# A Perceiver layer pair on one core: the first feed-forward as one program that reads 16-bit integers, the first cross attention merged with the norm of its latents, its tail keys on two halves of the array

## The chip, the cores and the metric

The kernel runs on one core of a Trainium2 chip. The metric is the device time of one execution in microseconds, as the median of several runs. Five engines take part: TensorE (PE in the profile, its weight loads PEld), VectorE (DVE), ScalarE (ACT), GpSimd (POOL) and SyncE (SP), which here only issues transfers.

## The reference, cut to what matters

The input x has 128 batches of 32 tokens with 128 features, the context 128 batches of 257 rows of 128. Six blocks follow one another, each added to x:

```python
x = x + L0_xattn(ctx, layernorm(x), mask)     # 16 heads of 64, keys = context AND latents
x = x + L0_attn(layernorm(x))                 # gated linear recurrence
x = x + L0_ffn(layernorm(x))                  # feed-forward with quantised activations
x = x + L1_xattn(layernorm(x), ctx, mask)     # 16 heads of 8
x = x + L1_attn(layernorm(x))
x = x + L1_ffn(layernorm(x))                  # experts and a shared expert
```

The two that the change touches:

```python
# first cross attention: the latents are normalised again and appended to the context
kv = concatenate([layer_norm(ctx, g1, b1), layer_norm(latents, g2, b2)], axis=1) @ Wkv   # 257 + 32 keys
weight = softmax(where(mask, q @ k.T * 64**-0.5, -big));  out = (weight @ v) @ Wout

# first feed-forward
def act_qdq(x):                                # one scale for the whole tensor
    scale = max(max(abs(x)) / 32767, 1e-12)
    return clip(round(x / scale), -32768, 32767) * scale
x = act_qdq(x)
up, gate = act_qdq(x @ wu.T), act_qdq(x @ wg.T)        # 128 -> 384
sig = clip(round(sigmoid(gate) * 65536), 0, 65535) / 65536
gate = act_qdq(gate * sig);  o = act_qdq(gate * up)
return o @ wd.T                                        # 384 -> 128
```

Each `act_qdq` needs the maximum over everything before the first element can be rounded, so the feed-forward has four points at which all work waits for one number.

## The kernel before

The tokens lie in a tile x of 128 partitions and 32 tiles of 128 features; a chunk is 4 tiles (512 columns), so there are 8 chunks. The stages run one after the other. Each stage is one or several blocks; in a block every engine has a program of its own, ordered by semaphores, and at a block's end all engines meet.

**First cross attention, `xattn0`.** It begins with `xattn0_inputs` (L448): `ln_stats` (L74) computes mean and scale for the 32 tiles and for the context's last row, as a block of its own. A second block then goes over the 8 chunks: VectorE and ScalarE normalise two tiles each (L480, L528), TensorE turns them and ScalarE writes `latT` (L534); VectorE multiplies by g2 (L486), GpSimd adds b2 (L501), and SyncE stores the result to memory (L557), from where it comes back as values. Then the block of the attention starts. GpSimd clears five tiles there (L681 to L686) and VectorE waits for that. Every engine next runs `step(g, j)` for each batch (`run_steps`, L431): 7 lead-in steps, the first 8 batches written out, a loop over 14 groups of 8 batches, the last 8 batches written out. A step works on several batches at once, for instance scores for batch s + 3 and values for batch s.

Per batch TensorE computes the scores (L853: 4 groups of 4 heads, 3 passes, 290 columns), a quarter of the next queries (L879), the product of probabilities and values over two context key tiles (L863) and over the third tile of keys, the tail (L870: the 32 latents and the last context row, spread over 128 partitions, most of them zero), and two transposes (L907). Every fourth batch it projects a finished tile (L895). VectorE masks the scores and takes the minimum (L728), transposes the probabilities in 32x32 blocks (L739 the two context tiles, L741 the tail), and does the context's norm (L755, L762, L769) and low halves (L773, L786). ScalarE takes the exponential and normalises (L801, L809) and copies out of PSUM (L819, L834, L838). GpSimd does scale and shift of the norm (L694 to L702) and, once a tile, the keys of the tail and the mask's bias (L709 to L716). SyncE spreads the transposed blocks over the partitions (L648, 4 transfers a batch) and loads raw context (L635) and tail values (L665, L667).

**First feed-forward, `ffn0`** (L1223). It is a chain of blocks, most of them with loops. (a) `layer_norm_T` (L136): VectorE normalises, TensorE turns, ScalarE copies into yT. `tensor_scale` (L1180) takes the maximum over all 4096 columns (L1196), turns it into a row, and forms step and inverse. (b) ScalarE multiplies by the inverse and adds the rounding constant RNE (L1259), VectorE takes it off and multiplies by the step (L1294), the result is split in a high and a low part (L1270, L1321), TensorE forms gate and up in 3 passes (L1332), ScalarE copies them (L1278), VectorE takes maxima (L1301). (c) Per item of 1024 columns, 12 items: ScalarE scales the gate (L1350), GpSimd subtracts RNE (L1370), ScalarE takes the sigmoid (L1356), VectorE rounds it (L1381), multiplies (L1385) and takes the maximum (L1389). (d) ScalarE scales up and gate (L1411, L1412), GpSimd subtracts RNE from up (L1421), VectorE multiplies (L1429) and takes the maximum (L1434). (e) ScalarE scales (L1457), VectorE dequantises (L1480), TensorE multiplies by the down weights (L1508), ScalarE copies, TensorE turns back (L1520), VectorE adds to x (L1488) and takes statistics.

## Time and profile before

| | before |
|---|---|
| runs, us | 1985.6, 1988.06, 1990.55; median 1988.06 |
| profiled execution, us | 1983.28 (span 1981.5) |
| PE / PEld busy | 1701.8 (86%) / 1391.9 (70%) |
| DVE / ACT / POOL busy | 1593.8 (80%) / 1490.9 (75%) / 889.3 (45%) |
| mean granted TensorE clock | 0.927 of 2.4 GHz |
| DMA | 261.67 MB, mean 132 GB/s |

Busy times are sums over the span. As the stages follow one another and differ in what leads them, a share of the whole says little; the stretches of the section on rows are cut at the stages. In timelines the first number is the start in us from the span's beginning, the second the length of the piece, and brackets hold the idle time before it and what ended it. Matmul pieces overlap by their tails, so the distance from start to start is what one costs.

### The profile page before, as it was taken

Reading aid. Unit: us, or ns where it says so; the run is one execution under the profiler, and the core shown is the slowest. Engines: PE = TensorE matmul, PEld = TensorE weight load, DVE = VectorE, ACT = ScalarE, POOL = GpSimd, SP = SyncE. Lnnn points to the kernel's source line nnn. Section 1 sums busy time; section 2 is a strip of 40 time slices with the busy share of each in tenths; the row PEclk is TensorE's granted clock in tenths of the full one; section 3 lists DMA queues with packets and bytes.
Section 4 is the critical chain, followed back from the end, with each engine's and each line's share of the span. In section 5 each row is a group of like instructions: output and inputs, shape, how many; then the busy total and the mean of one; then the engine's idle time right before and its main releaser. Section 6 shows DMA issues by size and latency. Waiting matters only on the chain. (4 is left out here: it accounts for less than half of the span.)

```text
span 1981.5 us, 50909 instructions
## 1 busy us (share of the span) xinstructions
PE 1701.8 (86%) x13415; PEld 1391.9 (70%) x13415; DVE 1593.8 (80%) x5006; ACT 1490.9 (75%) x4152; POOL 889.3 (45%) x1335
## 2 busy tenths in 40 slices
PE   3599999999999999985530569999999889979997
PEld 3499999999999999973420246676666556667775
DVE  4798888888888888849688779999999778866664
ACT  3588888888888888857576469999999778855553
POOL 1654444444444444412145224444444367725554
PEclk8699999999999999997675789999999889969998
DMA  4366666666666666640000039999999710016555
GB/s 139 94 167 163 161 161 161 161 161 161 161 161 161 161 162 162 162 114 0 0 0 0 0 102 247 252 250 249 249 249 249 194 33 0 1 28 100 102 96 107
DMA packets 224924, 261.67 MB, mean 132 GB/s; under 512 B 25144, under 2 KB 178268, under 8 KB 224720
## 3 DMA queue, kind: packets, MB, share of 16 engines
q1 hardware_dynamic: 223366, 258.64, 52.9%
q10 hardware_dynamic: 1194, 1.58, 0.3%
q8 instruction: 33, 0.54, 0.1%
q0 software_dynamic: 288, 0.56, 0.1%
q14 instruction: 43, 0.35, 0.1%
HBM read 88.19 MB, written 4.74 MB: 47 GB/s over the span
## 5 line engine op out<-in xcount | busy, mean ns | idle before, releaser
L863 PE MATMUL a_out<-a_probT,a_xn 128*128 128x256 f32 x1024 | 264.5, 382 | 4.2 <-DMA a_probT<-a_blocks 3.4
L801 ACT ACTIVATE a_prob<-a_neg,a_nmax 128x289 f32<-128x289 f32 x512 | 266.8, 526 | 1.3 <-DVE a_nmax L728 1.0
L694 POOL TENSOR_TENSOR a_xn<-a_z,g 128x256 f32<-128x256 f32 x128 | 94.0, 734 | 383.9 <-DVE a_z L762 383.9
L1767 ACT ACTIVATE b_prob<-b_neg,b_nmax 128x257 f32<-128x257 f32 x512 | 259.6, 512 | 5.8 <-DVE b_nmax L1702 5.1
L853 PE MATMUL a_score<-a_xnT,a_qT 128*128 128x290 f32 x1536 | 252.6, 314 | 1.1 <-DVE a_qT L773 1.1
L728 DVE CUSTOM_DVE_ANT_0 a_neg<-a_score,a_bias 128x289 f32<-128x289 f32 x512 | 211.4, 457 | 39.9 <-PE a_score L853 35.7
L809 ACT ACTIVATE a_prob<-a_prob,a_rinv 128x289 f32<-128x289 f32 x512 | 231.3, 528 | 1.8 <-DVE a_rinv L778 1.8
L853 PEld LDWEIGHTS a_score<-a_xnT,a_qT 128*128 128x128 f32 x1536 | 221.9, 190 | 7.9 <-issue 1.4
L1702 DVE CUSTOM_DVE_ANT_0 b_neg<-b_score,b_bias 128x257 f32<-128x257 f32 x512 | 188.4, 418 | 24.4 <-PE b_score L1872 17.0
L863 PEld LDWEIGHTS a_out<-a_probT,a_xn 128*128 128x128 f32 x1024 | 176.3, 192 | 19.2 <-DMA a_probT<-a_blocks 4.4
L739 DVE STREAM_TRANSPOSE a_blocks<-a_prob 128x1024 f32<-128x1024 f32 x128 | 159.4, 1245 | 22.5 <-ACT a_prob L809 16.0
L2438 POOL TENSOR_TENSOR m_hidden<-m_full,m_hidden 128x512 fp32r<-128x512 f32 (+1 forms) x88 | 113.7, 1292 | 109.1 <-ACT m_hidden L2397 109.1
L1713 DVE STREAM_TRANSPOSE b_blocks<-b_prob 128x1024 f32<-128x1024 f32 x128 | 156.4, 1222 | 1.2 <-ACT b_prob L1767 0.7
L879 PE MATMUL a_q<-latT,A 128*128 (+1 forms) x1024 | 139.5, 280 | 12.9 <-DVE a_qT L773 10.6
L879 PEld LDWEIGHTS a_q<-latT,A 128*128 128x128 f32 x1024 | 130.6, 196 | 14.7 <-DVE a_qT L773 12.0
L870 PE MATMUL a_out<-a_probT,a_tail 128*128 128x256 f32 x512 | 131.4, 379 | 0.0
L819 ACT ACTIVATE a_oT<-a_out 128x512 f32<-128x512 f32 x128 | 76.5, 598 | 71.6 <-PE a_out L870 71.6
L2392 ACT ACTIVATE m_silu<-m_g 128x512 f32<-128x512 f32 (+1 forms) x88 | 52.6, 597 | 92.1 <-PE m_g L2161 92.0
L895 PE MATMUL a_ctx<-U,a_oT 128*128 128x128 f32 x1024 | 119.7, 275 | 0.7 <-ACT a_oT L819 0.7
L895 PEld LDWEIGHTS a_ctx<-U,a_oT 128*128 128x128 f32 x1024 | 116.9, 192 | 1.1 <-ACT a_oT L819 1.1
L1673 POOL TENSOR_TENSOR b_last_part<-b_v_rows,b_prob 128x128 f32<-128x128 f32 x128 | 52.0, 406 | 129.0 <-ACT b_prob L1767 129.0
L870 PEld LDWEIGHTS a_out<-a_probT,a_tail 128*128 128x128 f32 x512 | 97.3, 190 | 13.2
(484 smaller groups left out, 4520.9 us busy)
## 6 DMA issues: line engine op xcount, KB each, us to landing
a_probT<-a_blocks SPq DMA_DIRECT2D x512, 192.0 KB, 3.4
b_probT<-b_blocks SPq DMA_DIRECT2D x256, 256.0 KB, 4.6
a_raw<-in_ctx SPq DMA_DIRECT2D x128, 128.0 KB, 3.0
b_raw<-in_ctx SPq DMA_DIRECT2D x64, 256.0 KB, 4.2
m_wide<-expert_weights SPq DMA_DIRECT2D x128, 128.0 KB, 6.8
a_kept<-keep SPq DMA_DIRECT2D x32, 257.0 KB, 3.4
b_kept<-keep SPq DMA_DIRECT2D x32, 257.0 KB, 4.7
b_v_rows<-ctx_tail_values SPq DMA_DIRECT2D x32, 256.0 KB, 4.7
```

The source lines that it names most:

```text
L728: nc.vector.tensor_tensor_reduce(out=neg[:, grp, :], in0=score_ps[grp][:, 0:KEYS0], in1=bias[:, n, :], scale=-DH0 ** -0.5, scalar=3.4e38, ...
L739: nc.vector.transpose(blocks[:, n, :, 0:2].rearrange("p r t g l -> p g r t l"), prob[:, n, :, 0:2 * P].rearrange("p g (r t c) -> p g r t c ...
L801: nc.scalar.activation(prob[:, par, grp, 0:KEYS0], neg[:, grp, :], ACT.Exp, bias=nmax[:, par, grp:grp + 1], scale=-1.0, accum_out=rsum[:, ...
L809: last = nc.scalar.activation(part, part, ACT.Copy, scale=rinv[:, j % 2, grp:grp + 1])
L853: last = nc.tensor.matmul(score_ps[grp][:, 0:even(KEYS0)], qT[:, a, un, bn, 4 * grp:4 * grp + 4, :], xnT[:, c, n, :], start=(p == 0), stop ...
L863: nc.tensor.matmul(out_ps[:, half, 0:2 * P], xn[:, j, kt, :], probT[:, u, 2 * half:2 * half + 2, kt, :], start=(kt == 0), stop=False)
L870: last = nc.tensor.matmul(out_ps[:, half, 0:2 * P], tail[:, j, :], probT[:, j % 2, 2 * half:2 * half + 2, 2, :], start=False, stop=True)
L879: last = nc.tensor.matmul(q_ps[:, h * P:(h + 1) * P], k.A[:, 4 * hg + h, :], k.latT[:, ds((t + ahead) * P, P)], start=True, stop=True)
L895: last = nc.tensor.matmul(proj_ps, oT[:, slot, :], k.U[:, slot % GROUPS * HG + slot // GROUPS, :], start=(slot == 0), stop=(slot == H - 1))
L1702: nc.vector.tensor_tensor_reduce(out=neg[:, par, grp, :], in0=score_ps[grp][:, 0:N_CTX], in1=bias[:, n, :], scale=-DH1 ** -0.5, scalar=3.4 ...
L1713: nc.vector.transpose(blocks[:, n, :, j % 2].rearrange("p r t g l -> p g r t l"), prob[:, j % 4, :, 0:2 * P].rearrange("p g (r t c) -> p g ...
L1767: nc.scalar.activation(prob[:, (j + 5) % 4, grp, :], neg[:, par, grp, :], ACT.Exp, bias=nmax[:, par, grp:grp + 1], scale=-1.0, accum_out=r ...
```

## The change

1. **Tail keys on two halves.** The 33 tail keys stand twice, in partitions 0 to 63 and again in 64 to 127, the latents in two rows of every four. One half of the partitions serves each half of the heads, so both tail matmuls of a batch contract over 64 rows, each in its own half of the array. Both kinds of value matmuls now take as their columns 64 of each of 4 head blocks. VectorE transposes the tail's probabilities in two instructions of 192 elements with overlapping windows instead of one of 256, SyncE loads the tail tile with 5 transfers instead of 2. The slots of the heads in the projection follow (U's index).
2. **The norm of the latents inside the attention's block.** `xattn0_inputs` is gone. `ln_stats` takes a SyncE and a GpSimd program along (the first raw loads; the clearing, now of a third of `blocks`). The chunk work stands written out ahead of the steps, with four of the seven lead-in steps between chunks 1, 3, 5 and 7; its tiles lie in `oT`, its PSUM in `out_ps`.
3. **VectorE's loop placed.** `run_steps` can say where in the instruction memory the loop's first instruction stands; VectorE's of this stage stands at slot 0.
4. **The feed-forward as one block**, written out without loops. Where the rounded value was needed, engines read the low 16 bits of the 32-bit word (value plus RNE) as an integer; the passes that took RNE off are gone, except in part (b), where GpSimd does it for chunks 1 to 7. The step is applied where the products are copied (b) and at the end (e). Maxima are taken chunk by chunk; half of up's scaling moves into (c); the sigmoid's table is loaded ahead. In (e) the activations are the stationary operand, so the product comes out in x's layout, with no copy and no turning back.

```diff
-def run_steps(eng, step, lead, lag=0, rest=8):
+def run_steps(eng, step, lead, lag=0, rest=8, **place):
-    with eng.Fori(1, (B - rest) // 8) as g:
+    with eng.bass.Fori(1, (B - rest) // 8, engines=[eng.engine], **place) as g:
...
+        EARLY = {1: 1, 3: 2, 5: 3, 7: 4}
+        mean, root, twice = ln_stats(k, stack, "lat_ln", k.ctx_tail[:], first_loads, clear)
...
-                        sp.dma_start(tail[0:P:KEY_STEP, rows, :], k.lat_dram[...]).then_inc(tail_loaded[u], 16)
+                        for first in (0, P // 2):
+                            for r in range(2):
+                                sp.dma_start(tail[first + r:first + P // 2:KEY_STEP, rows, :], latents[r * (L // 2):(r + 1) * (L // 2)])\
+                                    .then_inc(tail_loaded[u], 16)
+                        sp.dma_start(tail[2:P:P // 2, rows, :], k.ctx_tail_dram[batches, :].unsqueeze(0).broadcast_to([2, BPT, D]))\
                             .then_inc(tail_loaded[u], 16)
...
+                sp.wait_ge(tail_scaled, 2)
+                sp.dma_start(k.ctx_tail_dram, last_row[:, 1, :]).then_inc(tail_stored, 16)
+                for c in range(CHUNKS):
+                    sp.wait_ge(affine_ready, c + 1)
+                    sp.dma_start(k.lat_dram[c * CH:(c + 1) * CH, :].rearrange("(t p) d -> p t d", p=P), lat[:, c % 2]).then_inc(stored[c % 2], 16)
+                sp.wait_ge(z_ready, 1)
+                load_raw(sp, 0, 4)
+                for u in range(2):
+                    sp.wait_ge(stored[u], CHUNKS // 2 * 16)
+                run_steps(sp, step, LEAD - 2)
...  (GpSimd)
+                for c in range(CHUNKS):
+                    pool.wait_ge(lat_scaled, c + 1)
+                    nc.gpsimd.tensor_tensor(lat[:, c % 2], lat[:, c % 2], wide4(k.b2), ALU.add).then_inc(affine_ready, 1)
+                    if c in EARLY:
+                        step(-1, EARLY[c])
+                pool.wait_ge(lat_copied, CHUNKS)
+                run_steps(pool, step, LEAD - len(EARLY))
...  (VectorE)
-                    nc.vector.transpose(blocks[:, n, 0:2, 2].rearrange("p r g l -> p g r l"),
-                                        prob[:, n, :, 2 * P:2 * P + 2 * L].rearrange("p g (r c) -> p g r c", c=L)).then_inc(blocks_ready, 1)
+                    for half in range(2):
+                        pair = slice(2 * half, 2 * half + 2)
+                        last = nc.vector.transpose(blocks[:, n, 0:3, 2, pair].rearrange("p r g l -> p g r l"), tail_windows(n, half))
+                    last.then_inc(blocks_ready, 1)
...
+                    last.then_inc(z2_ready, 1)
+                    wait(dve, stored[u], c // 2 * 16)
+                    dve.wait_ge(z2_ready, c + 1)
+                    dve.wait_ge(z2_act, c + 1)
+                    nc.vector.tensor_tensor(lat[:, u], z2[:, u], wide4(k.g2), ALU.mult).then_inc(lat_scaled, 1)
...
+                run_steps(dve, step, LEAD - len(EARLY), LAG, head_slot={dve.engine: 0})
...  (TensorE)
-                        nc.tensor.matmul(out_ps[:, half, 0:2 * P], xn[:, j, kt, :], probT[:, u, 2 * half:2 * half + 2, kt, :],
+                        nc.tensor.matmul(out_ps[:, half, 0:2 * P], xn[:, j, kt, :], probT[:, u, :, kt, half * (P // 2):(half + 1) * (P // 2)],
...
-                        last = nc.tensor.matmul(out_ps[:, half, 0:2 * P], tail[:, j, :], probT[:, j % 2, 2 * half:2 * half + 2, 2, :],
-                                                start=False, stop=True)
+                        part = slice(half * (P // 2), (half + 1) * (P // 2))
+                        last = nc.tensor.matmul(out_ps[:, half, 0:2 * P], tail[part, j, :], probT[part, j % 2, :, 2, part], start=False, stop=True)
...  (ffn0, new)
+        def low(t):
+            return t.bitcast(I16).rearrange("p (n two) -> p n two", two=2)[:, :, 0]
...  ScalarE
+                def sigmoid(n):
+                    wait(act, gs_ready, n - SLOTS + 1)
+                    act.wait_ge(g_scaled, n + 1)
+                    nc.scalar.activation(part[:, n % SLOTS, :], low(item(all_gate, n)), ACT.Sigmoid, scale=step_of(UG, 1)).then_inc(sig_ready, 1)
...
+                for c in ACT_SCALES[1:]:
+                    scale_y(c)
+                for c in range(CHUNKS):
+                    if c + 1 < CHUNKS:
+                        upper_half(c + 1)
+                    for n, t, ps, w in sides:
+                        for j in range(FB0):
+                            act.wait_ge(done[n], c * FB0 + j + 1)
+                            nc.scalar.activation(chunk(t[:, j], c), ps[j][:], ACT.Copy, scale=step_of(Y)).then_inc(copied[n], 1)
+                nc.scalar.activation(sig_table[:], k.zero[:], ACT.Sigmoid)
+                act.wait_ge(scale_ready, UG + 1)
+                scale_gate(0)
+                scale_gate(1)
+                for n in range(ITEMS):
+                    sigmoid(n)
+                    if n + 2 < ITEMS:
+                        scale_gate(n + 2)
+                    if n % 2:
+                        scale_up(n // 2)
...  GpSimd
+                for c in range(1, CHUNKS):
+                    pool.wait_ge(y_hi, c + 1)
+                    nc.gpsimd.tensor_tensor(chunk(yT, c), chunk(yT, c), k.minus_rne[:].broadcast_to([P, CH]), ALU.add).then_inc(y_clean, 1)
+                    pool.wait_ge(y_clean, c)
+                    nc.gpsimd.tensor_tensor(y[:, LO, c * CH:(c + 1) * CH], chunk(yT, c), y[:, HI, c * CH:(c + 1) * CH], ALU.subtract)\
+                        .then_inc(y_lo, 1)
...  VectorE
+                def multiply_gate(n):
+                    dve.wait_ge(sig_rounded, n + 1)
+                    nc.vector.scalar_tensor_tensor(item(all_gate, n), part[:, n % SLOTS, :], -SIG, low(item(all_gate, n)), ALU.add, ALU.mult)\
+                        .then_inc(gs_ready, 1)
...
+                    nc.vector.tensor_tensor(item(all_up, n), low(item(all_gate, n)), low(item(all_up, n)), ALU.mult).then_inc(o_ready, 1)
...
+                    nc.vector.tensor_scalar(o, low3(o), step_of(O), None, ALU.mult).then_inc(o_dve, 1)
...  TensorE
+                def down(c):
+                    pe.wait_ge(o_dve, c + 1)
+                    pe.wait_ge(o_act, c + 1)
+                    wait(pe, added, c - 2)
+                    for n in range(4):
+                        t = c * 4 + n
+                        for j in range(FB0):
+                            last = nc.tensor.matmul(up_ps[c % 3][:, n * P:(n + 1) * P], up[:, j, t * P:(t + 1) * P], k.f_down[:, j, :],
+                                                    start=(j == 0), stop=(j == FB0 - 1))
```

## Rows read from the trace of the kernel before

**Rows 1.** Busy time by stretch: PE, PEld, DVE, ACT, POOL (instructions), then clock.
```profile
38.60:103.70 65.10, 34.75 (x165) 29.08 (x166) 47.38 (x147) 35.88 (x87) 35.27 (x55) 0.61 0.31 88
110.00:860.00 750.00, 749.73 (x5062) 706.02 (x5061) 646.94 (x2350) 622.64 (x1814) 351.87 (x662) 1.00 0.66 161
946.00:968.10 22.10, 9.21 (x33) 5.91 (x33) 16.03 (x48) 5.00 (x9) 0.00 (x0) 0.50 0.00 1
968.10:1013.30 45.20, 35.45 (x146) 28.58 (x146) 34.64 (x31) 37.64 (x66) 10.31 (x8) 0.88 0.00 0
1013.30:1066.30 53.00, 0.48 (x1) 0.18 (x1) 44.85 (x43) 28.54 (x25) 27.25 (x12) 0.50 0.00 0
1066.30:1109.10 42.80, 0.48 (x1) 0.18 (x1) 35.52 (x33) 27.27 (x24) 31.95 (x12) 0.50 0.00 0
1109.10:1144.70 35.60, 28.23 (x80) 13.29 (x80) 22.61 (x48) 17.33 (x16) 0.00 (x0) 0.88 0.00 1
```

**Rows 2.** Timeline of TensorE in the first attention's loop: start, length, operation.
```profile
506.69 1.03 PE L870 MATMUL a_out<-a_probT,a_tail 128*128 128x256 f32 x4
507.37 1.97 PE L853 MATMUL a_score<-a_xnT,a_qT 128*128 128x290 f32 x12
...
512.69 2.00 PE L853 MATMUL a_score<-a_xnT,a_qT 128*128 128x290 f32 x12
...
520.73 3.74 PE L895 MATMUL a_ctx<-U,a_oT 128*128 128x128 f32 x32
```

**Rows 3.** Timeline of TensorE in the second attention's loop.
```profile
1302.15 0.72 PE L1835 MATMUL b_score<-b_kT,b_qbd 32*128 32x257 f32 x8
1302.80 0.70 PE L1856 MATMUL b_k<-b_turned_in,wk1T 128*128 128x256 f32 x2
1303.33 0.38 PE L1864 MATMUL b_in<-ident,b_raw 128*128 128x128 f32 x2
```

**Rows 4.** Timeline of TensorE in the setup, two products of 64 rows.
```profile
26.98 0.27 PE L410 MATMUL setup_ps<-wk0T,wq0T 64*128 64x128 f32 x1
26.98 0.27 PE L410 MATMUL setup_ps<-wout,wv0T 64*128 64x128 f32 x1
```

**Rows 5.** Timeline of VectorE in the first attention's loop.
```profile
510.18 1.25 DVE L739 STREAM_TRANSPOSE a_blocks<-a_prob 128x1024 f32<-128x1024 f32 x1 [0.19 <-ACT a_prob L809]
511.35 0.40 DVE L741 STREAM_TRANSPOSE a_blocks<-a_prob 128x256 f32<-128x256 f32 x1
...
524.62 0.29 DVE L782 TENSOR_TENSOR x<-a_ctx,x 128x128 f32 x1 [0.50 <-PE a_ctx L895]
```

**Rows 6.** Timeline of GpSimd before the first attention's loop.
```profile
59.05 1.31 POOL L501 TENSOR_TENSOR lat_affine<-lat_affine,b 128x512 f32<-128x512 f32 x1 [0.95 <-DVE lat_affine L486]
...
76.35 0.29 POOL L709 CAST a_xnT<-latT 128x128 fp32r<-128x128 f32 x1
...
78.74 0.72 POOL L694 TENSOR_TENSOR a_xn<-a_z,g 128x256 f32<-128x256 f32 x1
...
83.77 0.71 POOL L702 TENSOR_TENSOR a_rstd<-a_var,minus_half 128x2 f32<-128x2 f32 x1
```

**Rows 7.** Timeline of VectorE in the first feed-forward.
```profile
962.12 4.42 DVE L1196 TENSOR_REDUCE f_y_scale<-f_yT 128x1 f32<-128x4096 f32 x1 [2.39 <-PEq L144]
...
1041.24 1.25 DVE L1381 TENSOR_SCALAR f_part<-f_part 128x1024 f32<-128x1024 f32 x1
1042.41 1.21 DVE L1385 SCALAR_TENSOR_TENSOR f_gate<-f_part,f_gate 128x1024 f32 x1
...
1054.41 0.68 DVE L1381 TENSOR_SCALAR f_part<-f_part 128x1024 f32<-128x1024 f32 x1
...
1077.43 1.78 DVE L1429 SCALAR_TENSOR_TENSOR f_up<-f_gate,f_up  x1
```

**Rows 8.** Timeline of TensorE in the first feed-forward.
```profile
973.32 4.14 PE L1332 MATMUL f_up<-f_y,f_w_up 128*128 x9 [5.99 <-POOL f_y L1321]
...
1112.71 7.62 PE L1508 MATMUL f_down<-f_up,f_downT 128*128 x12 [4.84 <-DVE f_up L1480]
```

More of the change, by code:

```diff
@@ L1358, in _, with norm @@
-                for n in range(-2, 3):
-                    step(n, n % 3)
-                with act.Fori(1, ITEMS // 3 - 1) as g:
-                    for u in range(3):
-                        step(g * 3 + u, u)
-                for n in range(ITEMS - 3, ITEMS):
-                    step(n, n % 3)
+                def norm(c):
+                    for j in (2, 3):
+                        t = c * 4 + j
+                        last = nc.scalar.activation(z[:, t * D:(t + 1) * D], k.x[:, t * D:(t + 1) * D], ACT.Identity,
+                                                    bias=offset[:, t:t + 1], scale=rstd[:, t:t + 1])
+                    last.then_inc(z_act, 1)
@@ new lines, in _ @@
+                act.wait_ge(inv_ready, 1)
+                nc.scalar.activation(rstd[:], inv[:], ACT.Sqrt).then_inc(root_ready, 1)
+                act.wait_ge(offset_ready, 1)
+                norm(0)
+                norm(1)
+                for c in range(CHUNKS):
+                    act.wait_ge(turned, c + 1)
+                    nc.scalar.activation(chunk(yT, c), ln_ps[c % 2][:], ACT.Copy).then_inc(yT_copied, 1)
+                    if c + 2 < CHUNKS:
+                        norm(c + 2)
@@ new lines, in statistics @@
+                def statistics(c):
+                    dve.wait_ge(added, c + 1)
+                    for n in range(4):
+                        last = tile_stats(k, c * 4 + n)
+                    last.then_inc(x_stats_ready, 1)
+                norm_chain()
+                for c in range(CHUNKS):
+                    norm(c)
+                    if c >= 2:
+                        max_y(c - 2)
+                max_y(CHUNKS - 2)
+                max_y(CHUNKS - 1)
+                dve.wait_ge(y_maxed, CHUNKS)
@@ new lines, in _ @@
+                find_scale(Y, y_max[:].unsqueeze(1))
+                dve.wait_ge(scale_ready, Y + 1)
+                scale_y(DVE_SCALES[0])
+                dve.wait_ge(y_hi, 1)
+                nc.vector.tensor_tensor(y[:, LO, 0:CH], low(chunk(yT, 0)), y[:, HI, 0:CH], ALU.subtract).then_inc(y_lo0, 1)
+                for c in DVE_SCALES[1:]:
+                    scale_y(c)
+                for c in range(CHUNKS):
+                    max_side(0, c)
+                    max_side(1, c)
+                dve.wait_ge(maxed, 2 * CHUNKS)
@@ L1512, in _, with turn @@
[L1512 to L1521 removed]
+                def turn(c):
+                    pe.wait_ge(z_ready, c + 1)
+                    pe.wait_ge(z_act, c + 1)
+                    wait(pe, yT_copied, c - 1)
+                    for j in range(4):
+                        t = c * 4 + j
+                        last = nc.tensor.transpose(ln_ps[c % 2][:, j * P:(j + 1) * P], z[:, t * D:(t + 1) * D], k.ident[:])
+                    last.then_inc(turned, 1)
@@ new lines, in turn_rows, with products @@
+                def turn_rows(i):
+                    pe.wait_ge(chain[i], 2)
+                    for t in range(scale[i].shape[2]):
+                        last = nc.tensor.transpose(rows_ps[:, t * P:(t + 1) * P], rows[:, t, :], k.ident[:])
+                    last.then_inc(rows_turned, 1)
+                def products(c):
+                    if c == 0:
+                        pe.wait_ge(w_lo, 2)
+                        pe.wait_ge(y_lo0, 1)
+                    else:
+                        pe.wait_ge(y_lo, c)
+                    for n, t, ps, w in sides:
+                        for j in range(FB0):
+                            wait(pe, copied[n], (c - 1) * FB0 + j + 1)
+                            for p, (a, b) in enumerate(PASSES):
+                                last = nc.tensor.matmul(ps[j][:], w[:, a, j * P:(j + 1) * P], y[:, b, c * CH:(c + 1) * CH],
+                                                        start=(p == 0), stop=(p == len(PASSES) - 1))
+                            last.then_inc(done[n], 1)
@@ L1524, in xattn1 @@
+                for c in range(CHUNKS):
+                    turn(c)
+                turn_rows(Y)
+                for c in range(CHUNKS):
+                    products(c)
+                turn_rows(UG)
+                turn_rows(GS)
+                turn_rows(O)
+                for c in range(CHUNKS):
+                    down(c)
 def xattn1(k, io):
```

712 lines of the change are left out of this document (302 added, 410 removed).

## Prediction

> **What bounds the kernel now.** I read the page's slices first, then the windows by stage, and in each stage the timeline of the engine without gaps. The profiled execution took 1983.28 us around a span of 1981.5; 4.8 us below the median of the runs shown (1988.06), so I work out a difference and take it from the median. The reader should see three stages [rows 1]. From 38.6 to 103.7 nothing is full: the latents' norm is a program of its own, with the attention's lead-in behind it. From 110 to 860 TensorE is busy 749.73 of 750 us at the 2.4 GHz level: the first attention's loop is TensorE's. From 946.0 to 1144.7 lies the first feed-forward, five stretches in which VectorE or ScalarE leads, TensorE only in the second and last.
>
> In the loop a batch takes 5.32 us (score to score, 507.37 to 512.69), and every fourth has 32 projection matmuls as well, 3.74 with the tail of the last, 3.57 without it, so 0.112 each [rows 2]: 24.85 us a tile of four batches, 32 tiles. VectorE is close behind: per ordinary batch it waits only 0.2 for ScalarE, so its own work is about 5.17; once a tile it waits 0.50 and more [rows 5].
>
> **Part 1, tail keys on two halves (TensorE).** Now: 4 instructions (2 matmuls, 2 instructions each, as all f32 here) of 0.216, from 506.69; the fourth streams until 507.55: 0.86 us a batch [rows 2]. After: the two matmuls hold 64 rows each, in different row groups. That such streams run side by side shows in the setup, where two 64-row products start together at 26.98 [rows 4]. So the stretch has two rounds, 2 x 0.216 = 0.43. But the shape changes twice. The second attention does that each batch: eight 32-row instructions of 257 columns take 0.65 from their start to the next start (1302.15 to 1302.80), two rounds of 0.217 plus 0.21 of weight load and emptying; the 128-row pair behind them takes 0.53 to its successor where two cost 0.43 [rows 3], 0.10 for its bare weight load. What the entry costs beyond the stretch's own first load no row gives alone; I take 0.08, an emptying like the one behind it. Sum 0.65 + 0.10 + 0.08 = 0.83 against 0.86: 0.03 saved, times 128 = -4 us. Bounds: no entry cost, 0.75 (-14 us); entry as dear as load and emptying together, 0.95 (+11). 0.83 lies nearest to the rows.
>
> The page "TensorEngine Tiling (Array Packing)" of the Trainium skill (Key Properties) says that changing the mode drains TensorE, while its section Theoretical Speedup gives up to 2x for a contraction of 64. By the 2x alone a batch would save 0.43; but then VectorE (below) holds ordinary batches at 5.36 and the loop gains 9 us, not 4. By the drain, the trace agrees, 0.1 and a bare weight load per change [rows 3].
>
> **VectorE's share.** The 256-element transpose (0.40) becomes two of 192. From the 1024 one (1.25) and the 256 one, an element costs 1.11 ns and an instruction 0.12, of which some 0.07 overlaps the next [rows 5]: 2 x 0.26 instead of 0.33, +0.19. Its ordinary batch is then 5.36, above TensorE's 5.29, and it falls behind 0.07 a batch; three batches make 0.2, with its own 0.19 some 0.4, against the 0.50 it waits before the tile's addition [rows 5]. So it catches up once a tile and costs nothing; cover 0.1 us a tile. Below: nothing gained, as TensorE leads. Above: the lag isn't recovered, rival A. Where VectorE's loop starts in its instruction memory changes no row I can price: no gap stands at the loop's edge; 0, up to 1 us in each of 14 turns either way.
>
> SyncE issues five tail loads a tile for two, some 0.5 us each more, 1.5 us, in the batch before the projection, where it has 8.9 us for four instructions of spreading, some 0.7 each by estimate; the bytes go from 66 to 132 KB per 24.85 us, beside 161 GB/s [rows 1]. Hidden; if not, the loads of raw context come 1.5 late with several us in hand.
>
> **Part 2, the latents' norm merged.** Now POOL adds a bias for 8 chunks (1.31 each, with a pause of 0.95 before it), then clears tiles, and only then does the lead-in begin; POOL ends its fourth lead-in step at 83.77 + 0.71 = 84.48 [rows 6]. After: the clearing lies beside the statistics chain, and four steps lie between the chunks. POOL becomes the merged block's bound: from 46.95, 8 x 1.30 = 10.4; four variance-and-power pairs at 0.95 = 3.8; three products-and-sums at 1.5 = 4.5; the tile keys from 76.35 to 78.74, 2.4 [rows 6]; waits on VectorE 1.5. It ends at 69.6 instead of 84.5: -15. TensorE's cold clock (0.5 for most of this stage) hurts less than POOL. Late next is SyncE: its tail loads and the fifth raw tile wait until the last latents are stored, about 69.4, so raw 5 lands near 75.5, just when it is wanted. Bounds: -17 (VectorE's own chain), -11 (SyncE late by 4).
>
> **Part 3, the feed-forward.** The integers are read as the low 16 bits, so neither POOL nor VectorE takes the rounding constant away; five blocks become one.
> (a) 946.0 to 968.1, 22.1 us: the 4.42 reduction over 4096 elements becomes a maximum per chunk, of which the last 0.6 stays, and the 2.39 before it shrinks by a block's edge, 1.2 [rows 7]. -4.9.
> (b) 45.2 us: the first product starts at 973.32, after 5.99 idle [rows 8]; then it stands 2.2 after the scale, for 5.2 now. The 144 matmuls behind it are TensorE's (busy 35.45 of 45.20 [rows 1]) and stay, 16 groups of nine; ScalarE's copies take the scale along free, its chunk about 3.8 < 4.08, POOL's now two passes 2.5. With the edge: -4.1.
> (c) 53.0 us: POOL's subtraction goes. Where it runs, VectorE's rounding takes 1.25, and with the product and the maximum at 1.17 + 2 x 1.13 = 3.43 an item; where it has ended the same takes 0.68, so 2.86 [rows 7] (an instruction of 1.21 frees the engine after 1.13: 1041.24 + 1.17 = 1042.41). Then 12 x 2.86 = 34.3, filling 6.9 (ScalarE: two scalings, sigmoids in line), scale 2.2: 43.4. ScalarE per item, an estimate from its 28.54 busy for 25 instructions [rows 1], 1.13 + 1.06 + half of a 1.13 scaling of up = 2.75, under VectorE's. -9.6.
> (d) 42.8 us: the product took 1.78 beside POOL; free it is 1.13, as is the maximum [rows 7]. 12 x 2.26 = 27.1, start 1.3, scale 2.4: 30.8. ScalarE, 27.27 busy for 24 of its scalings now [rows 1], has 18, 20.4, hidden. -12.0.
> (e) 35.6 us: no copy and no turning back; 24 instructions a chunk at 0.112 = 2.69, VectorE by my estimate 1.13 + 0.6 + 0.82 = 2.55. 8 x 2.69 = 21.5; 2.9 to the first product, 2.0 lost at the 1.2 GHz level until the clock rises (it rose 4.5 us after 1112.71 [rows 8]), 1.5 at the end: 27.9. -7.7.
> Sum -38.3. The trace of before has no 16-bit read with stride: below, nothing gained over f32; above, half rate on 24 products (+25, rival B). I take the f32 rate, that of the same elements. Bounds without that: -31 (fills and scales 1.5 longer in each part), -44 (ScalarE and VectorE overlap fully).
>
> **Sum.** -4 - 15 - 38.3 = -57.3: 1983.3 becomes 1926.0, and on the median 1930.8, say 1930. Its own range: 1988 - 75 = 1913 to 1988 - 31 = 1957, rarely at both ends together; 1914 to 1950.
>
> **Rivals.**
> A. VectorE becomes the loop's bound: ordinary batches at 5.44 and the lag carried over. For it: 0.1 us of cover a tile. Against: waits of over 1 us behind the addition in the projection batch. Tile 3 x 5.44 + 8.88 = 25.20, +0.35 x 32 = +11 instead of -4: 1946.
> B. The strided 16-bit reads run at half rate: +1.07 on 24 products and some on the last stretch: 1961. For it: no row. Against: no element more is read.
> C. The merged start is bound elsewhere (SyncE's wait for the stores, ScalarE's alternate work): 5 saved for 15: 1940.
> D. Slower: the two halves don't overlap on the same accumulation, and both shape changes cost 0.32 (the 0.21 of load and emptying and the 0.10 of a bare load, together, at each). The tail stretch is 0.86 + 0.64 = 1.51, +0.65 x 128 = +83, less 53: 2018. It decides from 1.28 us a stretch. Against it: rows 3 and 4.
> E. The change does less than it says: POOL leaves the feed-forward, but VectorE's rounding stays at 1.25. Then (c) saves 3, not 9.6: 1937.
>
> **Chances.** Forecast 0.60, A 0.16, C 0.09, E 0.05, B 0.06, D 0.04. The range 1910 to 1952 holds the forecast's own, A, C and E, leaving B, D and tails out. Faster by over 0.3% (6 us, about what a measurement of this kernel tells from none) 0.93, within it 0.03, slower 0.04.
>
> **What would show it.** Tail stretch, values' end to first score: near 0.83; near 0.5 means no drain, above 1.28 D. TensorE full from about 95 to 855, a tile 24.7; if VectorE is full and TensorE has gaps in the loop, A. Lead-in's fourth POOL step ends near 70. Feed-forward 199 to about 160, VectorE's rounding 0.68 throughout, its product 1.2 (B: 2.3). Wrong: a loop turn above 50.5 us, or a feed-forward above 172.

## The result and the profile after

The changed kernel took 1940.21 us (median of 4 runs, 1938.02 to 1943.30), the kernel before 1988.30 in the same session. The ratio is 0.976 with a 95% interval of 0.9741 to 0.9778: 48 us faster, where 58 were forecast. Both the profiled executions lie below their medians, 1938.02 (span 1936.2) and 1983.28 (span 1981.5), 45.3 apart.

The ends of the blocks on VectorE cut both spans into stages:

| stage | before | after | difference | forecast |
|---|---|---|---|---|
| setup, to 37.2 / 36.6 | 37.2 | 36.6 | -0.6 | 0 |
| first attention, to 889.5 / 876.4 | 852.3 | 839.8 | -12.5 | -19 |
| recurrence, to 944.9 / 932.5 | 55.4 | 56.1 | +0.7 | 0 |
| first feed-forward, to 1144.7 / 1096.5 | 199.8 | 164.0 | -35.8 | -38.3 |
| second attention, to 1587.8 / 1539.9 | 443.1 | 443.4 | +0.3 | 0 |
| second recurrence, to 1743.9 / 1696.1 | 156.1 | 156.2 | +0.1 | 0 |
| second feed-forward, to the end | 237.6 | 240.1 | +2.5 | 0 |

The same stretches as in [rows 1], first the attention's start, then its loop, then the five parts (a) to (e) of the feed-forward (busy time of PE, PEld, DVE, ACT, POOL with their instructions, then clock, DMA share, GB/s):

```profile
36.60:93.00 56.40, 32.12 (x167) 28.28 (x168) 44.79 (x141) 34.50 (x80) 34.61 (x54) 0.66 0.32 92
110.00:840.00 730.00, 730.00 (x4970) 627.46 (x4969) 645.28 (x2421) 614.98 (x1771) 344.77 (x650) 1.00 0.67 164
932.50:951.90 19.40, 8.94 (x33) 5.99 (x33) 14.22 (x41) 11.76 (x27) 1.95 (x2) 0.50 0.00 0
951.90:993.80 41.90, 35.52 (x146) 28.38 (x146) 31.29 (x26) 38.80 (x63) 16.34 (x14) 0.91 0.00 1
993.80:1037.05 43.25, 0.47 (x1) 0.18 (x1) 36.06 (x43) 33.06 (x30) 0.00 (x0) 0.50 0.00 0
1037.05:1067.86 30.81, 0.47 (x1) 0.18 (x1) 28.73 (x33) 20.48 (x18) 0.00 (x0) 0.50 0.00 0
1067.86:1096.50 28.64, 23.75 (x192) 23.59 (x192) 17.38 (x49) 18.36 (x16) 0.00 (x0) 0.88 0.00 1
```

TensorE is busy 730.00 of 730 us: the loop is still its own, so rival A (VectorE sets its pace) did not come. GpSimd is gone from (c) and (d). In the loop, TensorE's timeline (start, length) answers to [rows 2] and VectorE's to [rows 5]:

```profile
501.35 0.70 PE L847 MATMUL a_out<-a_probT,a_tail 64*128 64x256 f32 x4
501.98 1.86 PE L829 MATMUL a_score<-a_xnT,a_qT 128*128 128x290 f32 x12
...
507.25 1.88 PE L829 MATMUL a_score<-a_xnT,a_qT 128*128 128x290 f32 x12
...
516.10 1.88 PE L829 MATMUL a_score<-a_xnT,a_qT 128*128 128x290 f32 x12
```

```profile
510.07 1.25 DVE L675 STREAM_TRANSPOSE a_blocks<-a_prob 128x1024 f32<-128x1024 f32 x1 [0.16 <-ACT a_prob L767]
511.24 0.59 DVE L679 STREAM_TRANSPOSE a_blocks<-a_prob 128x192 f32<-128x192 f32 x2
...
513.74 0.29 DVE L720 TENSOR_TENSOR x<-a_ctx,x 128x128 f32 x1 [0.23 <-PE a_ctx L871]
```

A batch takes 507.25 - 501.98 = 5.27 for 5.32, so rival D (0.65 more a batch) did not come either. A turn of eight takes (828.56 - 137.05) / 14 = 49.39 for 49.71. VectorE's wait before the tile's addition fell from 0.50 to 0.23: it falls behind a little in each ordinary batch and has caught up by the end of the tile.

GpSimd ahead of the loop (its fourth lead-in step ends at 74.91 + 0.71 = 75.62; [rows 6] had 84.48) and VectorE there:

```profile
55.11 1.30 POOL L645 TENSOR_TENSOR a_oT<-a_oT,b 128x512 f32<-128x512 f32 x1 [2.51 <-DVE a_oT L745]
...
74.91 0.71 POOL L619 TENSOR_TENSOR a_rstd<-a_var,minus_half 128x2 f32<-128x2 f32 x1
```

```profile
53.05 0.69 DVE L711 TENSOR_TENSOR a_qT<-a_q,a_qT 128x512 fp32r<-128x512 f32 x1 [2.02 <-ACT a_qT L792]
53.65 0.59 DVE L739 TENSOR_SCALAR a_oT<-x,lat_ln_mean,lat_ln_twice 128x128 f32<-128x128 f32 x2
...
75.43 0.46 DVE L658 CUSTOM_DVE_ANT_0 a_neg<-a_score,a_bias 128x289 f32<-128x289 f32 x1 [1.06 <-issue]
```

In the feed-forward, VectorE answers to [rows 7] and TensorE to [rows 8]:

```profile
1005.62 0.68 DVE L1419 TENSOR_SCALAR f_part<-f_part 128x1024 f32<-128x1024 f32 x1
1006.22 1.22 DVE L1423 SCALAR_TENSOR_TENSOR f_gate<-f_part,f_gate 128x1024 f32<-128x1024 f32 x1
1007.35 1.21 DVE L1428 TENSOR_REDUCE f_gs_max<-f_gate 128x1 f32<-128x1024 f32 x1
1008.48 0.68 DVE L1419 TENSOR_SCALAR f_part<-f_part 128x1024 f32<-128x1024 f32 x1
...
1039.57 1.22 DVE L1433 TENSOR_TENSOR f_up<-f_gate,f_up 128x1024 f32<-128x1024 int16 x1
```

```profile
954.28 4.18 PE L1536 MATMUL f_up_ps<-f_y,f_w_up 128*128 128x512 f32 x9 [3.09 <-DVE f_y L1467]
958.26 2.47 PE L1536 MATMUL f_gate_ps<-f_y,f_w_gate 128*128 128x512 f32 x9
960.57 2.20 PE L1536 MATMUL f_up_ps<-f_y,f_w_up 128*128 128x512 f32 x9
...
1070.46 23.75 PE L1547 MATMUL f_up_ps<-f_downT,f_up 128*128 128x128 f32 x192 [3.81 <-DVE f_up L1442]
```

The item is 1008.48 - 1005.62 = 2.86, as forecast.

### The profile page after: what moved, and what is told of

The parts are those of the page before. It is cut to its first block and busy times, and to the rows that moved or that the text cites. A ratio compares the mean times of both kernels' runs of the same rounds, so it can differ in the third digit from the quotient of the medians.

```text
span 1936.2 us, 50375 instructions
## 1 busy us (share of the span) xinstructions
PE 1690.7 (87%) x13527; PEld 1332.0 (69%) x13527; DVE 1581.4 (82%) x5121; ACT 1505.8 (78%) x4166; POOL 837.8 (43%) x1319
## 5 line engine op out<-in xcount | busy, mean ns | idle before, releaser
L829 PE MATMUL a_score<-a_xnT,a_qT 128*128 128x290 f32 x1536 | 241.4, 306 | 1.2 <-DVE a_qT L711 1.1
L829 PEld LDWEIGHTS a_score<-a_xnT,a_qT 128*128 128x128 f32 x1536 | 210.9, 189 | 42.7 <-issue 42.7
L1806 ACT ACTIVATION_READ_ACCUMULATOR b_prob<-b_neg,b_nmax 128x1 f32 x512 | 104.6, 204 | 0.0
L2031 POOL TENSOR_TENSOR s_spread<-s_keys,head_of_feature 128x1536 f32<-128x1536 f32 x32 | 88.8, 2776 | 34.7 <-ACT s_keys L2125 34.7
```

Source lines behind the costliest of these rows:

```text
L829: last = nc.tensor.matmul(score_ps[grp][:, 0:even(KEYS0)], qT[:, a, un, bn, 4 * grp:4 * grp + 4, :], xnT[:, c, n, :], start=(p == 0), stop ...
L1806: nc.scalar.activation(prob[:, (j + 5) % 4, grp, :], neg[:, par, grp, :], ACT.Exp, bias=nmax[:, par, grp:grp + 1], scale=-1.0, accum_out=r ...
```

## The experiments

All are edits of the changed kernel. Where it says "in one run", the kernel ran once, with the profiler; the others have 4 or 5 runs. Where a stage is given, it is from the profiles. Most stages repeat far better than whole runs: where its code is unchanged the feed-forward took 163.3 to 165.2 us. The second attention, whose code is the same everywhere, took 441.9 to 451.4, so whole times that differ by a few us say little.

**1. Without the placement of VectorE's loop.**

```diff
-                run_steps(dve, step, LEAD - len(EARLY), LAG, head_slot={dve.engine: 0})
+                run_steps(dve, step, LEAD - len(EARLY), LAG)
```

> The changed kernel without the placement of VectorE's loop in the first attention. My theory: the loop is TensorE's (730.00 of 730 us busy from 110 to 840), VectorE catches up once a tile, so the time stays at 1938 to 1943, a turn of 8 batches stays 49.39 (two tiles of 24.68 or 24.70), and at most a gap of under 1 us appears on VectorE at the loop's edge. Rival: the placement is what made a turn 0.32 shorter than before (49.71); then a turn is 49.7 here and the time 5 us longer.

Measured: 1976.56 us (1974.36 to 1979.41), 36 us longer. Both my theory and its rival were wrong: it is far more than either. What VectorE waited for from 190 to 830 (total, times, longest), and the place in one turn:

```profile
DVE a_neg L658 <- issue: 38.8, 13, 3.7
```

```profile
501.55 0.17 DVE L716 RECIPROCAL a_rinv<-a_rsum 128x4 f32<-128x4 f32 x1
501.63 0.39 DVE L724 TENSOR_TENSOR a_xnT<-a_ctx,a_xnT 128x256 fp32r<-128x256 f32 x1
505.12 0.46 DVE L658 CUSTOM_DVE_ANT_0 a_neg<-a_score,a_bias 128x289 f32<-128x289 f32 x1 [3.09 <-issue]
```

Thirteen gaps of 3.0 on average, with no releaser: 14 turns have 13 jumps back. The trace's records of the jump itself show where the time goes: the next instruction of VectorE's sequencer starts 3.4 to 4.2 us behind each jump back, and the two instructions shown ahead of the gap had been issued before the jump. In the changed kernel, and in the one before, it starts 0.3 to 0.4 behind. The changed kernel has no line of "issue" in that stretch. A turn lasts 51.7 to 54.0 us for 49.39: VectorE cannot make up for it in two tiles, and TensorE waits for its masks.

**2. The loop at slot 236** (`head_slot={dve.engine: 236}` for 0).

> The changed kernel with VectorE's loop placed at slot 236 instead of slot 0. Without any placement VectorE stood still for 2.8 to 3.7 us once in each turn, just behind the loop's edge, with nothing it waited for that the profile shows, and the time was 36 us longer. The body has 283 instructions, in the kernel before it had 275. Theory: what counts is whether the body lies in two or in three stretches of 256 slots; from 236 it ends at 518, in the third, so the gap is back: 14 gaps of about 3 us, 30 to 40 us longer, 1970 to 1980. Rival (any stated placement helps, by the branch that it puts ahead of the loop or by a better entry): no gaps, 1938 to 1943.

Measured in one run: 1984.23 us; the gaps are back (13 of them, 35.6 us in all), and a turn is (875.4 - 139.0) / 14 = 52.60, 3.2 more. The theory holds, its price was set somewhat low. A second, smaller gap appears inside the body in 9 of the turns, some twenty instructions behind its first, about where slot 256 lies:

```profile
403.29 0.46 DVE L658 CUSTOM_DVE_ANT_0 a_neg<-a_score,a_bias 128x289 f32<-128x289 f32 x1 [2.63 <-issue]
...
406.85 0.38 DVE L679 STREAM_TRANSPOSE a_blocks<-a_prob 128x192 f32<-128x192 f32 x1 [0.54 <-issue]
```

**3. No slot, but a hint for the back edge.**

```diff
-                run_steps(dve, step, LEAD - len(EARLY), LAG, head_slot={dve.engine: 0})
+                run_steps(dve, step, LEAD - len(EARLY), LAG, hint_back_edge=True)
```

> The changed kernel without placement of VectorE's loop, but with a hint for its back edge, armed at the top of each turn. Without either, VectorE stood 2.8 to 3.7 us in each turn and the time was 36 us longer. Theory (the stretch of instructions that the jump goes to is fetched only when the jump is taken): the hint has it fetched earlier, the gaps shrink below 1 us and the time is 1938 to 1950. Rival (the gap lies in a third stretch of 256 slots that has to be fetched anyway, whatever is said of the jump): the gaps stay near 3 us and the time near 1976.

Measured in one run: the line "issue" is absent from VectorE's waits between 190 and 830, the next instruction of the sequencer starts 0.24 to 0.31 behind the jump, the 14 turns last (829.1 - 137.6) / 14 = 49.39, and the attention ends at 876.0 (876.4 in the changed kernel). The whole run took 1945.56, mostly since its second attention, the same code, took 449 instead of 443. So the gap is the late fetch of the instructions that the jump goes to.

The page "Runtime: NRT & Kernel Launch" of the Trainium skill (Instruction fetch mechanics) says that the instruction memory of most engines is two blocks of 256 instructions, and that a taken branch to a place outside them has to wait for a fetch. By that rule a body of 283 is free while it touches two blocks and pays when it touches three: the runs agree (slot 0, none; slot 236, whose body ends at 518, about 3 us a turn). At which slot the unplaced loops begin, here and in the kernel before, no run shows.

**4. The tail as before.** 128 rows, one transpose of 256, two loads a tile:

```diff
-                        part = slice(half * (P // 2), (half + 1) * (P // 2))
-                        last = nc.tensor.matmul(out_ps[:, half, 0:2 * P], tail[part, j, :], probT[part, j % 2, :, 2, part], start=False, stop=True)
+                        last = nc.tensor.matmul(out_ps[:, half, 0:2 * P], tail[:, j, :], probT[:, j % 2, 2 * half:2 * half + 2, 2, :],
+                                                start=False, stop=True)
...
```

> The changed kernel with the tail as before: 128 rows in both tail matmuls, one transpose of 256, two tail loads a tile; everything else as changed. My theory: the halves run side by side and the changes of shape eat most of it; what is left is 0.04 to 0.05 a batch. So a turn goes back from 49.39 to 49.71, the time rises by 5 us (1945), and the attention's start is unchanged. Rival (the gain in the loop is VectorE's placement): a turn stays 49.39 and the time 1940. Second rival (the tail halves gained more, VectorE's longer work gave it back): the turn is then above 49.71.

Measured: 1945.08 (1944.28 to 1948.10), 4.9 longer; a turn is (833.6 - 137.6) / 14 = 49.71, as in the kernel before, and the first attention as a whole is 5.3 longer. The theory holds.

**5. Both tail products on rows 0 to 63** (the second then takes the first half's keys).

```diff
-                        part = slice(half * (P // 2), (half + 1) * (P // 2))
+                        part = slice(0, P // 2)
```

> The changed kernel, where both tail products use rows 0 to 63, so that they cannot lie beside each other; count and size of the instructions are the same (the second half then takes the first half's tail keys). My theory: side by side they need two rounds of 0.31 us, one behind the other four of 0.216, plus the two changes of shape: 0.2 to 0.45 us more a batch, so a tile takes 25.5 to 26.4 instead of 24.7, and the attention 25 to 55 us longer: 1965 to 1995. Rival (the gain of the loop comes from elsewhere, the two halves never overlapped in what bounds it): under 0.05 a batch, the time within 6 us.

Measured in one run: 1995.43. The batch is 526.57 - 520.86 = 5.71, 0.44 more, a turn 52.82:

```profile
519.80 1.13 PE L847 MATMUL a_out<-a_probT,a_tail 64*128 64x256 f32 x4
520.86 1.89 PE L829 MATMUL a_score<-a_xnT,a_qT 128*128 128x290 f32 x12
...
525.52 1.13 PE L847 MATMUL a_out<-a_probT,a_tail 64*128 64x256 f32 x4
526.57 1.89 PE L829 MATMUL a_score<-a_xnT,a_qT 128*128 128x290 f32 x12
```

0.43 is two instructions of 0.216: the overlap is real and worth 0.43 a batch. Without it a batch is 5.71 - 5.32 = 0.39 longer than in the kernel before; that is what the shape changes cost, and 0.04 is left. The page "TensorEngine Tiling (Array Packing)" of the Trainium skill, weighed in the prediction, says both; the changes of shape take nine tenths of the gain.

**6. Merged start: VectorE normalises the next chunk before its lead-in step.**

```diff
+                    if c + 1 < CHUNKS:
+                        norm_half(c + 1)
                     if c in EARLY:
                         step(-1, EARLY[c])
```

> The changed kernel, with VectorE's normalisation of the next chunk of latents issued ahead of its part of the lead-in step, instead of behind it. In the changed kernel each pair of chunks takes 7.0, 6.2 and 7.1 us, GpSimd is idle 2.5 us in the first, and VectorE waits 2.0, 0.9 and 0.9 us for ScalarE's copy of the queries before it touches the next chunk. My theory (the merged start is bound by a ring: VectorE's normalisation, TensorE's transposes and queries at the 1.2 GHz level, ScalarE's copy, VectorE's low half, then the next normalisation): the pairs shrink by 1 to 2 us each, the first mask comes 3 to 5 us earlier (75.43 becomes 70.5 to 72.5), the time falls to 1935 to 1937. Rival (GpSimd bounds it, as I forecast): the first mask moves by less than 0.5 us and the time stays.

Measured: 1940.24 (1937.74 to 1945.82); the first mask at 74.69, or 37.8 after the stage's start for 38.8 (38.5 to 39.2 in the nine profiles with the unchanged start). Between the two forecasts: the waits for the queries shrank to 0.55, 0 and 0.46, but VectorE then met the next limit, the transfer that empties its buffer:

```profile
64.66 0.41 DVE L724 TENSOR_TENSOR a_xnT<-a_ctx,a_xnT 128x256 fp32r<-128x256 f32 x1
68.06 0.91 DVE L750 TENSOR_TENSOR a_oT<-a_oT,g 128x512 f32<-128x512 f32 x1 [2.99 <-DMA latents_normalised<-a_oT]
```

**7. The same with four buffers** (in `probT`, which is idle then).

```diff
-        z2, lat = oT[:, 0:8].rearrange("p (u t) d -> p u t d", u=2), oT[:, 8:16].rearrange("p (u t) d -> p u t d", u=2)
+        z2 = oT[:, 0:8].rearrange("p (u t) d -> p u t d", u=2)
+        lat = probT[:].rearrange("p u i t q -> p (u i t) q")[:, 0:16].rearrange("p (u t) d -> p u t d", u=4)
...
-                    wait(dve, stored[u], c // 2 * 16)
+                    wait(dve, stored[c % 4], c // 4 * 16)
```

> The kernel of the experiment in which VectorE normalises the next chunk first, with four buffers for the latents on their way to memory instead of two. There VectorE stood 2.99 us (65.07 to 68.06) until the transfer of chunk 4 had left its buffer, and that transfer had waited for GpSimd, which was 6 us in a lead-in step with the tile's keys. Theory: the merged start was held by three things of nearly equal length, the ring over VectorE, TensorE and ScalarE first, this buffer next; with both gone the first mask comes at 70.5 to 71.5 instead of 74.7 (and 75.4 in the changed kernel), 3 to 4 us off the time. Rival (GpSimd's own queue, which stays as it is, ends last): the first mask at 73.5 or later.

Measured in one run: 1938.61, the first mask at 75.36: nothing gained, the rival holds. That wait is gone, and GpSimd's fourth step still ends at 75.11 + 0.71 = 75.8. From 62.00 to 75.62 GpSimd is busy 12.95 of 13.62 in both kernels; from 46.95 to 62.00 VectorE is now busy 14.15 of 15.05, drawn out by GpSimd:

```profile
66.08 1.78 DVE L751 TENSOR_TENSOR a_probT<-a_oT,g 128x512 f32<-128x512 f32 x1
67.79 1.54 DVE L741 TENSOR_SCALAR a_oT<-x,lat_ln_mean,lat_ln_twice 128x128 f32<-128x128 f32 x2
69.42 0.69 DVE L751 TENSOR_TENSOR a_probT<-a_oT,g 128x512 f32<-128x512 f32 x1
...
70.72 2.51 DVE L701 TENSOR_SCALAR a_z<-a_raw,a_mv,a_rstd 128x128 f32<-128x128 f32 x2 [0.22 <-POOL a_rstd L620]
```

The same product takes 0.69 or 1.78. A pair of the latents' normalisations takes 0.59 undisturbed and 1.54 here, the context's pair 0.58 in the loop and 2.51 here. GpSimd's pass beside that product ran from 66.06 to 67.31, and the product ended 0.55 later.

**8. GpSimd at work beside part (c)**, with 16 passes that nothing reads.

```diff
+                pool.wait_ge(scale_ready, UG + 1)
+                for n in range(16):
+                    nc.gpsimd.tensor_tensor(item(yT, 0), item(yT, 0), k.minus_rne[:].broadcast_to([P, W]), ALU.add).then_inc(beside, 1)
+                    pool.wait_ge(beside, n + 1)
```

> The changed kernel with 16 additions of 1024 columns on GpSimd beside part (c) of the feed-forward; nothing reads their result. My theory: VectorE's rounding of the sigmoid takes 0.68 now because GpSimd is idle, and 1.25 where it runs. Each GpSimd pass takes about 2.2 us here, so 16 last 36 of the 43 us: some 10 of the 12 roundings take 1.25, part (c) goes from 43.25 to 48.5 to 50, the product and maximum stay at 1.22 and 1.21. Rival (0.68 comes from the new layout of the work, not from GpSimd): the roundings stay 0.68 and part (c) 43.25.

Measured in one run: 1963.38; the feed-forward took 180.3 instead of 164.0. Most roundings take 1.25 as expected, but the product, expected unchanged, is 2.91 instead of 1.22. Below are four instructions of VectorE and the pass of GpSimd beside them:

```profile
1016.86 1.25 DVE L1423 TENSOR_SCALAR f_part<-f_part 128x1024 f32<-128x1024 f32 x1
1018.03 2.91 DVE L1427 SCALAR_TENSOR_TENSOR f_gate<-f_part,f_gate 128x1024 f32<-128x1024 f32 x1
1020.87 1.21 DVE L1432 TENSOR_REDUCE f_gs_max<-f_gate 128x1 f32<-128x1024 f32 x1
1022.00 1.25 DVE L1423 TENSOR_SCALAR f_part<-f_part 128x1024 f32<-128x1024 f32 x1
```

```profile
1017.64 2.22 POOL L1346 TENSOR_TENSOR f_yT<-f_yT,minus_rne 128x1024 f32<-128x1024 f32 x1
```

The product starts at 1018.03, within a pass that ends at 1017.64 + 2.22 = 1019.86, and ends 1.08 after it, about its own undisturbed time. Every product that starts within a pass does so, and every rounding ends 0.55 after the pass in which it started. The 1.25 is therefore no slower form of the rounding but 0.7 of waiting and a short form behind it; the one at 1005.47 met a longer rest and took 2.38. In turn a pass that meets the product takes 2.75 instead of 2.22.

**9. The same, where the product reads 32-bit words** (`item(all_gate, n)` for `low(item(all_gate, n))`).

> The experiment with 16 GpSimd passes beside part (c), where the product also reads its second operand as full 32-bit words instead of the low 16 bits. With the 16-bit read the product took 2.91 beside GpSimd and 1.22 without it; in the kernel before, the f32 product took 1.21 beside GpSimd's subtraction. Theory (it is the strided 16-bit read that loses beside GpSimd): the product goes back to 1.21 to 1.25, the rounding stays 1.25, part (c) is 48 to 50. Rival (any product of two streams loses beside this GpSimd pass, which here writes and reads one place over and over): the product stays at 1.8 or more and part (c) at 53 or more.

Measured in one run (it computes other values): 1956.72, and the product still takes 2.91:

```profile
1011.08 2.91 DVE L1427 SCALAR_TENSOR_TENSOR f_gate<-f_part,f_gate 128x1024 f32<-128x1024 f32 x1
```

So it is not the 16-bit read; the rival holds. The 16 passes take 39.26 us, 2.45 each, in both experiments, and VectorE's item of experiment 8, 1022.00 - 1016.86 = 5.14, is two passes and a little: the product waits out the pass it meets. In [rows 7] the same product took 1.21, though GpSimd ran there too. The trace of the kernel before shows why: from 1028 on each product of part (c) starts in a pause of GpSimd (at 1042.41, the next pass at 1042.95). The one that started within a pass took 2.91 there too, and the rounding behind it 2.38:

```profile
1023.19 2.18 POOL L1370 TENSOR_TENSOR f_gate<-f_gate,minus_rne 128x1024 f32 x1
1023.54 2.91 DVE L1385 SCALAR_TENSOR_TENSOR f_gate<-f_part,f_gate 128x1024 f32<-128x1024 f32 x1
1026.38 2.38 DVE L1381 TENSOR_SCALAR f_part<-f_part 128x1024 f32<-128x1024 f32 x1
```

The page "SBUF — State Buffer" of the Trainium skill (Who interferes with whom; two separate sides) says that VectorE and GpSimd share a pair of ports that one of them locks for its whole instruction, whoever starts first, VectorE only for instructions with two inputs in SBUF or in its fast modes for copies and operations with a scalar. The traces agree: product and rounding wait for the end of the pass they meet, the maximum keeps 1.21 within one, and in the kernel before the products that started first kept 1.21.

**10. VectorE reads 32-bit words in (c), (d) and (e)**, GpSimd idle.

> The changed kernel, where VectorE's two products and its last scaling read the full 32-bit words instead of their low 16 bits with a stride of two (the numbers are then others, the count of elements is the same). My theory: a 16-bit read with stride costs VectorE what a 32-bit read costs, 1.22 for 1024 elements; parts (c), (d) and (e) keep 43.2, 30.8 and 28.6 within 0.3 us, the last scaling of 1024 may fall from 0.75 to 0.69. Rival (16-bit operands are dearer or cheaper than they look): the products move by more than 0.1 us each, 2.4 us or more in all.

Measured in one run (it computes other values): 1945.59, the feed-forward 163.7 (164.0 in the changed kernel), its product still 1.22:

```profile
1039.84 1.22 DVE L1433 TENSOR_TENSOR f_up<-f_gate,f_up 128x1024 f32<-128x1024 f32 x1
```

A 16-bit read with stride costs what a 32-bit one does. The longer time lies in the second attention, whose code is the same: 451.4 for 443.4.

**11. Products that nothing reads, ahead of (b) and (e).**

```diff
+                def busy(n):
+                    for _ in range(n):
+                        nc.tensor.matmul(gate_ps[0][:, 0:FF0], w_up[:, HI, 0:P], w_up[:, HI, :], start=True, stop=True)
...
+                busy(5)
                 turn_rows(Y)
+                busy(8)
...
                 turn_rows(GS)
+                pe.wait_ge(o_maxed, 8)
+                busy(36)
                 turn_rows(O)
+                busy(11)
```

> The changed kernel with products on TensorE that nothing reads, in the feed-forward's waits ahead of its two product stretches: 5 of 384 columns behind the last transpose and 8 behind the first scale's, 36 in the later half of the third stretch and 11 behind its scale's. In the changed kernel the first group of nine products takes 3.98 us to the next, at clock 0.50, where a later one takes 2.04, and the last stretch runs at 0.50 until 1074.5. My theory (the clock follows what TensorE did before): the first group takes 2.0 to 2.5, the last stretch is 2 us shorter, in all 3 to 4 us: 1936 to 1937. Rival (in both places ScalarE's scaling leads, not TensorE, so the clock is hidden): less than 1 us.

Measured: 1935.80 (1931.43 to 1939.00), ratio to the kernel before 0.9743 (0.9727 to 0.976); the feed-forward took 160.7 for 164.0. The first group of nine is 2.16 to the next for 3.98, and the last stretch runs at clock 1.00:

```profile
954.33 2.32 PE L1536 MATMUL f_up_ps<-f_y,f_w_up 128*128 128x512 f32 x9 [1.29 <-DVE f_y L1467]
956.49 2.20 PE L1536 MATMUL f_gate_ps<-f_y,f_w_gate 128*128 128x512 f32 x9
...
1069.25 21.68 PE L1547 MATMUL f_up_ps<-f_downT,f_up 128*128 128x128 f32 x192 [1.87 <-DVE f_up L1442]
```

**12. Experiments 7 and 11 together.**

> The changed kernel with next chunk first, four buffers and the products that nothing reads ahead of the two product stretches of the feed-forward. If the gains add, as they lie in stages that follow one another: 3.4 for the feed-forward and 4 for the start, so 1932 to 1934, faster than the changed kernel (1940) by 0.3 to 0.4%. Rival (an earlier start is lost again in the first attention's loop, where the transfers set the pace of the first turns): 1936 to 1938.

Measured: 1936.38 (1932.46 to 1939.28), ratio to the kernel before 0.9745 (0.9727 to 0.9763), no better than 11 alone, as 7 had brought nothing. Against the changed kernel's 0.976 (0.9741 to 0.9778) both gain about 0.2%, and the intervals overlap; only the stage, 3.3 us shorter in 11 and 2.6 in 12, is clear.

## Why the prediction was right, and where not

The three parts, their signs and their order of size were right; 1940 lies 10 above the forecast and inside the range.

**Part 1.** Forecast -4, measured -4.9 by taking it back (5.3 in the stage alone). The price of the shape changes was sized within 0.02 a batch, the overlap (experiment 5) and the catching up of VectorE came as described.

**Part 2 is the step that failed: -15 forecast, -8.0 at the first mask** (38.8 after the setup's end for 46.8), outside its own bounds of -17 and -11. The end of GpSimd's fourth step, which the forecast put near 70, came at 75.62. GpSimd was named as the bound, and its work was sized well: 10.4 + 3.8 + 4.5 + 2.4 = 21.1 forecast, 21.86 busy measured from 46.95 to 75.62. The term "waits on VectorE 1.5" was wrong: it waits 28.67 - 21.86 = 6.8, most of it before 62, where VectorE works in turns with TensorE at the 1.2 GHz level and ScalarE. Rival C had the size (1940), but its causes were only half right: undoing the ring (6) and then the buffer (7) left the first mask 1.0 and 0.1 earlier than in the changed kernel. The 0.1 is within the scatter of 38.5 to 39.2. What sets the pace up to 62.00 stays open; from there to 75.62 GpSimd is busy 12.95 of 13.62. The trace also shows that GpSimd's passes hold VectorE up, which a sum of undisturbed durations doesn't see: in the changed kernel ten of VectorE's normalisations and products in this stretch wait for a pass, some 5.7 us of its 22.59 busy (an estimate: what they took above their undisturbed 0.34 and 0.69).

**Part 3.** Forecast -38.3, measured -35.8: (a), from the stage's start, -3.8 for -4.9, (b) -3.3 for -4.1, (c) -9.8 for -9.6, (d) -12.0 for -12.0, (e) -7.0 for -7.7. The parts with a steady item were right within 0.2; the other three each missed by about 1, which was not traced further. Rival B fell with experiment 10, rival E with roundings of 0.68 to 0.70.

**The placement** was costed at nothing, at most 1 us in each of 14 turns. Against the kernel before that is what it did, but its true price was outside my bounds: without it the change would have been worth 12 us, not 48. That this term did no harm is the kernel's merit, not the forecast's. Before, neither the 275 instructions nor their place made a gap, so no row could show it. The count alone would not have shown it either, since 275 and 283 both exceed 256: the slot at which the body begins is needed too.

**Elsewhere**, 3.6 us came back in code that the change doesn't touch, less 0.6 in the setup. With 7.0 in part 2 and 2.5 in part 3, less 0.5 in the loop, that makes the 12 us between -57.3 and -45.3. The 3.6 are +0.7 in the first recurrence, where TensorE's low clock lasts a little longer (0.50 from 882 to 887, 0.63 in the same place before), +0.4 in the two stages of the second layer, and +2.5 in the last stage, where VectorE waits 7.0 us in 11 pieces for transfers of the experts' weights, the longest 2.4 (one of 0.3 before). The second attention took 441.9 to 451.4 us in fourteen profiles of the same code; why was not traced.

## What to carry over

Where a loop's body is longer than 256 instructions, look at the slot it begins at, and place the loop or hint its edge: an unplaced body of 283 instructions cost 36 us here. When a sum says one engine bounds a merged start, take the waits of its partners from rows too, and lengthen VectorE's products, roundings and normalisations wherever a pass of GpSimd is running when they start. Removing GpSimd's passes paid although GpSimd was not the bound, as VectorE no longer waited for them.

## What the runs showed of the hardware

- At each jump back VectorE stood still 2.6 to 3.7 us when the loop of 283 instructions began at slot 236 or unplaced, and not at all at slot 0 or with a hint.
- VectorE's product and rounding, started within a GpSimd pass of 1024 columns, wait for its end: the product takes up to 2.91 instead of 1.22, the rounding 1.01 to 2.38 instead of 0.68. The maximum stays at 1.21. A product that starts before the pass keeps 1.21. 16-bit or 32-bit makes no difference.
- Two products of 64 rows on different rows overlap fully, also where each adds to an accumulation that products of 128 rows began (0.43 a batch), and changing the shape twice eats all but 0.04.
- 13 short products in a wait before (b), and 47 before (e), raised TensorE's clock from 0.50 to 1.00 for what followed and took 3.3 us off the stage.
